# Banded attention: the output mix as three one-pass products of split operands, with the casts on VectorE and GpSimd

## The reference

```python
qkv = (x @ Wqkv.T + bqkv)            # 16 heads of 16; x is layer-normed, 1024 tokens, 256 wide
scores = einsum('bhncd,bhnld->bhncl', qc, kb) / sqrt(d)
attn = softmax(where(band, scores, -inf))
o = einsum('bhncl,bhnld->bhncd', attn, vb)   # weigh the values
return o @ Wout.T + bout             # the output mix; the caller adds x
```

## Time and profile before

| | us |
|---|---|
| runs of the kernel | 3609.21, 3608.74, 3601.73; median 3608.74 |
| the profiled execution | 3606.72 |
| its span in the profile | 3604.9 |
| of it `window_attention` | about 2846 to 3532 |

### The profile page before, as it was taken

One profiled execution on the slowest core, in us unless ns is written; L12 is line 12 of the kernel. 1 busy time (PEld: TensorE's weight loads), 2 busy tenths in 40 slices (PEclk: granted clock), 3 DMA queues, 4 the chain that ended last, 5 costly groups with the idle time before them and its releaser, 6 DMA issues. The chain is left out here.

```text
span 3604.9 us, 123855 instructions
## 1 busy us (share of the span) xinstructions
PE 3338.7 (93%) x48438; PEld 3008.6 (83%) x48438; DVE 2214.2 (61%) x6367; ACT 2105.8 (58%) x6623; POOL 1554.9 (43%) x2318
## 2 busy tenths in 40 slices
PE   8939999789957999899999999999998899999998
PEld 8929999777737999898999899899997677877877
DVE  6675555688775555545544444444444688888887
ACT  5546555455445555444444444444444499999996
POOL 5755565201024665344444444454444533333225
PEclk9969999899978999999999999999999899999999
DMA  4153343511134443500000000000000143333332
GB/s 129 48 169 85 89 97 56 159 48 51 52 136 135 91 95 67 144 3 3 3 3 3 3 3 3 3 3 3 3 3 6 52 129 115 101 105 104 105 96 99
DMA packets 202968, 234.47 MB, mean 65 GB/s; under 512 B 18065, under 2 KB 183073, under 8 KB 202401
## 3 DMA queue, kind: packets, MB, share of 16 engines
q1 hardware_dynamic: 177824, 192.99, 17.1%
q0 software_dynamic: 24576, 33.57, 5.6%
HBM read 147.46 MB, written 79.04 MB: 63 GB/s over the span
## 5 line engine op out<-in xcount | busy, mean ns | idle before, releaser
L2437 ACT ACTIVATE wa_S<-wa_S,wa_top 128x192 f32<-128x192 f32 x1024 | 459.6, 464 | 52.7 <-DVE wa_top L2502 52.6
L1956 DVE TENSOR_TENSOR so_raw<-so_rows,so_masks 128x1024 f32<-128x1024 f32 x256 | 313.5, 1225 | 228.6 <-PE so_rows L1655 219.7
L2035 POOL TENSOR_TENSOR so_more<-so_compact,so_head 128x384 f32<-128x384 f32 x224 | 185.2, 827 | 339.1 <-PE so_bankC L1737 308.4
L2502 DVE CUSTOM_DVE_ANT_0 wa_S<-wa_bank,wa_band 128x192 f32<-128x192 f32 x1024 | 299.5, 349 | 3.9 <-issue 3.9
L1945 DVE SCALAR_TENSOR_TENSOR so_compact<-so_compact,so_bankX 128x96 f32<-128x96 f32 x192 | 48.8, 254 | 355.6 <-PE so_bankX L1773 355.6
L2040 POOL TENSOR_TENSOR so_OT<-so_O,so_OT 128x128 fp32r<-128x128 f32 x256 | 116.9, 456 | 307.9 <-ACT so_OT L1876 307.9
L1870 ACT COPY so_O<-so_bankC 128x128 f32<-128x128 f32 x256 | 68.1, 266 | 308.1 <-PE so_bankC L1737 308.1
L650 POOL DMA_INDIRECT sum_dram<-y,rows x128 | 222.9, 1741 | 29.4 <-issue 27.3
L2348 PE MATMUL wa_bank<-ident,wa_S 128*128 128x128 f32 x1536 | 220.8, 277 | 8.0 <-ACT wa_probT L2444 5.4
L728 ACT ACTIVATE m2e_hT<-m_bank,m2e_bias 128x256 fp32r<-128x256 f32 x256 | 126.8, 495 | 149.7 <-PE m_bank L680 143.2
L728 ACT ACTIVATE m4e_hT<-m_bank,m4e_bias 128x256 fp32r<-128x256 f32 x256 | 126.3, 493 | 150.2 <-PE m_bank L680 145.0
(11 more groups left out here) (449 smaller groups left out, 10030.2 us busy)
## 6 DMA issues: line engine op xcount, KB each, us to landing
m_w_raw<-in_L_ffn_W_dram SPq DMA_DIRECT2D x64, 512.0 KB
wa_V<-wa_V_dram SPq DMA_DIRECT2D x256, 128.0 KB, 2.8
sum_dram<-X SPq DMA_DIRECT2D x16, 1024.0 KB, 4.8
X<-sum_dram SPq DMA_DIRECT2D x16, 1024.0 KB, 8.4
wa_V_dram<-wa_V_new SPq DMA_DIRECT2D x32, 512.0 KB, 4.1
wa_V_rest<-wa_V_dram SPq DMA_DIRECT2D x128, 128.0 KB, 3.0
X<-in_L_attn_a_x_dram SPq DMA_DIRECT2D x8, 1024.0 KB, 11.7
xn_dram<-m2r_xn SPq DMA_DIRECT2D x16, 512.0 KB, 4.5
```

Source lines behind the costliest of these rows:

```text
L1956: nc.vector.tensor_tensor(AB[:, t % 2].rearrange("p h m t -> p h (m t)"), rows4[:, :, 0:2 * P], masks[:].rearrange("p m t -> p (m t)")[:, ...
L2035: nc.gpsimd.tensor_tensor(state[:, t % UT], compact[:, t % UT, :, None, :].broadcast_to([P, 3, HG, DK]), head[:, None, :, None].broadcast_ ...
L2437: nc.scalar.activation(S[:, n % 2, z], S[:, n % 2, z], ACT.Exp, bias=top[:, n % 2, z:z + 1], scale=-1.0, accum_out=sums[:, i % 2, SET * c ...
L2502: nc.vector.tensor_tensor_reduce(out=S[:, n % 2, z], in0=bS[g][:, eo * SPAN:(eo + 1) * SPAN], in1=band[:], scale=-(D ** -0.5), scalar=3e38 ...
```

## The change

`woT` becomes a pair of `float32r` tiles, a high and a low part; the weights are loaded into a piece of `S` that isn't in use yet, ACT casts the high part after its items of the first batch and DVE subtracts for the low part after its own. PE waits for that (`w_ready` 3) before its first `scores`. `OT` becomes such a pair too. In `weighed` the product is written over `RT`; a third DVE instruction casts it to the high part, and a new instruction on POOL, `low_O`, subtracts for the low part; that one now gives `O_ready`. `weigh` waits for the new `O_read`. The mix is six `float32r` products (three pairs of parts, two chunks) in place of two float32 ones.

```diff
-        woT = sb("woT", [P, HC, HID])
+        woT = sb("woT", [P, 2, HC, HID], F32R)
...
-        wT_raw = S[:].rearrange("p a z k -> p (a z k)")[:, 0:HC * 3 * HID].rearrange("p (c r) -> p c r", c=HC)
+        raw_weights = S[:].rearrange("p a z k -> p (a z k)")
+        wT_raw = raw_weights[:, 0:HC * 3 * HID].rearrange("p (c r) -> p c r", c=HC)
+        woT_raw = raw_weights[:, HC * 3 * HID:HC * 4 * HID].rearrange("p (c r) -> p c r", c=HC)
...
-        OT = sb("OT", [P, 2, HC, P])
+        OT = sb("OT", [P, 2, 2, HC, P], F32R)
...
-                sp.dma_start(woT[:], R.outT_dram).then_inc(s_["out_loaded"], 16)
+                sp.dma_start(woT_raw, R.outT_dram).then_inc(s_["out_loaded"], 16)
...
+                def low_O(i):
+                    pool.wait_ge(s_["O_high"], i + 1)
+                    nc.gpsimd.tensor_tensor(OT[:, i % 2, 1].rearrange("p c t -> p (c t)"), RT,
+                                            OT[:, i % 2, 0].rearrange("p c t -> p (c t)").bitcast(F32), ALU.subtract).then_inc(s_["O_ready"], 1)
...
                         low_xT(position(b + 1, 2 * j))
+                    if 1 <= i <= NT:
+                        low_O(i - 1)
...
                     if c == 0 and i >= 1:
-                        pe.wait_ge(s_["O_ready"], i)
+                        pe.wait_ge(s_["O_read"], i)
...
                 def mix(i):
                     pe.wait_ge(s_["O_ready"], i + 1)
-                    for c in range(HC):
-                        last = nc.tensor.matmul(bO[:, HID:2 * HID], OT[:, i % 2, c], woT[:, c, :], start=(c == 0), stop=(c == HC - 1))
+                    steps = [(u, v, c) for u, v in PARTS for c in range(HC)]
+                    for n, (u, v, c) in enumerate(steps):
+                        last = nc.tensor.matmul(bO[:, HID:2 * HID], OT[:, i % 2, u, c], woT[:, v, c, :], start=(n == 0), stop=(n == len(steps) - 1))
...
-                pe.wait_ge(s_["out_loaded"], 16)
+                pe.wait_ge(s_["w_ready"], 3)
...
+                act.wait_ge(s_["out_loaded"], 16)
+                nc.scalar.copy(woT[:, 0], woT_raw).then_inc(s_["w_high"], 1)
...
                 def weighed(i):
                     dve.wait_ge(s_["RT_done"], i + 1)
+                    if i >= 1:
+                        dve.wait_ge(s_["O_ready"], i)
                     nc.vector.tensor_copy(RT, bO[:, HID:2 * HID]).then_inc(s_["RT_ready"], 1)
                     dve.wait_ge(s_["RT_ready"], i + 1)
-                    nc.vector.tensor_tensor(OT[:, i % 2].rearrange("p c t -> p (c t)"), bO[:, 0:HID], RT, ALU.mult
-                                            ).then_inc(s_["O_ready"], 1)
+                    nc.vector.tensor_tensor(RT, bO[:, 0:HID], RT, ALU.mult).then_inc(s_["O_read"], 1)
+                    dve.wait_ge(s_["O_read"], i + 1)
+                    if i >= 2:
+                        dve.wait_ge(s_["out_done"], i - 1)
+                    nc.vector.tensor_copy(OT[:, i % 2, 0].rearrange("p c t -> p (c t)"), RT).then_inc(s_["O_high"], 1)
...
+                dve.wait_ge(s_["w_high"], 3)
+                nc.vector.tensor_tensor(woT[:, 1], woT_raw, woT[:, 0].bitcast(F32), ALU.subtract).then_inc(s_["w_ready"], 1)
                 for n in range(SETS + 6):
```

More of the change, by code:

```diff
@@ L2138, in window_attention @@
         top, sums, share = sb("top", [P, 2, SET]), sb("sums", [P, 2, H]), sb("share", [P, 2, H])
-        OT = sb("OT", [P, 2, HC, P])
+        OT = sb("OT", [P, 2, 2, HC, P], F32R)
         names = """loaded qkv_loaded out_loaded zeroed V_zeroed V_edges step var_ready std_ready scaled xn_ready item_done act_item dve_item qm_ready S_done masked
-                   prob_ready T_done T_act T_dve PV_done share_ready share_spread RT_done RT_ready O_ready out_done y_ready
+                   prob_ready T_done T_act T_dve PV_done share_ready share_spread RT_done RT_ready O_read O_high O_ready out_done y_ready
                    x_ready w_high w_ready xT_low""".split()
```

## The result

| | us |
|---|---|
| before, median of 9 runs | 3606.35 (3601.73 to 3609.21) |
| changed, median of 9 runs | 3615.14 (3608.62 to 3616.61) |
| ratio, changed to before | 1.0024, 95% interval 1.0013 to 1.0034 |
| profiled executions | 3606.72 and 3615.26, spans 3604.9 and 3613.4 |

The change makes the kernel slower by 8.8 us, 0.24%, as forecast (3616; by the sum +9.3 us).

What follows compares the result with a forecast made beforehand. ACT was taken as the bound except in n = 8 to 15 of seven batches, bound by a closed DVE-PE loop. Loop 4.2, held cast 2.3, start 1.9 and end 0.93 gave +9.3 us, 3616 us; range 3604 to 3625.

Steps and rivals of the forecast that it cites:

- What bounds the stage: In n = 8 to 15 of seven batches, a closed loop of mix, DVE with `weighed`, `scores`, PE; elsewhere ACT.
- Rivals 3: DVE isn't the loop's tighter side: casts are free, the mix's gain stays; -1.9 us, 3604.8 us; chance 0.15.
- 4 (PE bounds everywhere): PE is the bound in every n and each of 64 mixes gains: -8 us, 3598.7 us; chance 0.05.
- The cast, +0.33 us: In `weighed`, a DVE cast of 0.29 us puts 0.33 us more on DVE ahead of the next mask.
- Rival 5: The cast runs at the one-to-one rate, 0.42 us; the mix gains only 0.11: +15 us, 3621.7 us; chance 0.15.
- The mix, -0.17 us: On PE, six `float32r` products take 0.85 us where the float32 mix took 1.02, a gain of 0.17 us.
- The loop, +4.2 us: In n = 8 to 15 of seven batches, each of 28 pairs of n grows by 0.15 us: +4.2 us.
- the held cast, +2.3 us: At n = 7, `low_xT` on POOL holds DVE's cast; 0.33 us reaches the mix of n = 8, seven times: +2.3 us.
- Rival 2: The cast isn't held by POOL: +7.0 us, 3613.7 us; chance 0.15.
- `low_O` on POOL, nothing: 64 subtractions of 0.73 us on POOL cost nothing, except at the very end.
- The start, +1.9 us: Before the first `scores`, the subtraction for the weights' low part delays the first mask; ACT bounds from there: +1.9 us.
- The end, +0.93 us: Cast and `low_O` make the last mix 1.10 us later, less 0.17 for the faster mix: +0.93 us.

Runs made afterwards that it cites:

- the cast alone: Kernel before plus one DVE cast of 128x256 behind the product of `weighed`, into a tile nobody reads; 3617.18 us beside 3606.28, ratio 1.0031.
- the mix alone: Changed kernel without cast and `low_O`, the product written straight to the high part, which all six products read; 3604.26 us beside 3606.28, ratio 0.9995.
- two products: Changed kernel with a second DVE product from PSUM writing the high part in place of the cast; 3611.97 us beside 3606.28, ratio 1.0015.
- the cast behind the masks: Changed kernel with the cast moved behind the eighth mask of the same n; 3605.27 us beside 3606.28, ratio 0.9997.
- the late subtraction at the start: Changed kernel with the weights' low-part subtraction behind the masks of n = 0, PE's wait at the first mix; 3612.56 us beside 3605.31, ratio 1.0015.

## Why the prediction was right, point by point

**What bounds the stage.** Right, and it is shown, not only argued: a cast added alone lengthens the pair by its 0.33 us, a second one by 0.16 of its 0.18, and the same cast behind the last mask by nothing. Rivals 3 (DVE has slack) and 4 (PE bounds everywhere) are refuted by the cast alone and the mix alone.

**The cast, +0.33 us.** Right to the hundredth: cast 0.294 us in n = 9 to 15. Rival 5 with its 0.42 us is refuted.

**The mix, -0.17 us.** It was -0.15: from the first start to the bias addition 0.91 us against 1.06. The products start 0.112 to 0.124 us apart in n = 8 to 14, 0.119 on average, where I took 0.113. A pair in the loop so costs 0.18 and not 0.15.

**The loop, +4.2 us, and the held cast, +2.3 us.** Together 6.5 were forecast. In the trace n = 8 to 15 of seven batches take 5.6 us more and the other n, the first apart, 0.7. How they divide is read from bias addition to bias addition. With two products, where nothing is held, the four steps of two n from n = 8 to 16 take 4.8 us more over seven batches than in the kernel before, but the step behind them (n = 16 to 18) takes 1.0 less, so that 3.9 us are left of the loop's term and not 28 x 0.18 = 5.0; that this lies so near 4.2 is partly luck, since the pair was sized too low and what comes back behind the loop was allowed for by rounding down only. In the changed kernel all these steps take 6.2 us more; the 2.3 between the two is the held cast. The held casts took 1.11 to 1.39 us, most of them less than the 1.3 to 1.5 that I had named; at n = 7 I had 1.45 for the mask's delay, and the row shows (3249.44 - 3247.94) - 0.35 = 1.15, since `low_xT` had started 0.3 us before the product's end. Even so the mix of n = 8 came 0.29 to 0.33 us later in six of the seven batches, counted from the first exponent of n = 7, and 0.59 in the first (0.33 forecast), and taking the holding away gave 2.5 us there. That the cast is held at all was an assumption there, from an instruction with two SBUF inputs; the two kinds of cast, 0.29 us alone and 1.11 or more beside `low_xT`, and the two products that nothing holds now show it. The Trainium skill, page "SBUF — State Buffer", section "SBUF: two separate sides", has this as an exclusive lock that a float32 copy between SBUF tensors takes too: the trace agrees, for a cast to `float32r` as well, and the one that waits ends some 0.15 us after the one that it waited for. Rival 2 is refuted.

**`low_O` on POOL, nothing.** Right: the kernel with the cast behind the masks has the same `low_O`, and its pair is as short as that of the mix alone. It counts at the end only, as forecast: PE waits for it once, 2.1 us, at the last tile.

**The start, +1.9 us.** The term that I mis-sized. The wait itself was +1.75, but 0.83 came back. Timelines of the changed kernel:

```profile
2879.91 0.68 DVE L2560 TENSOR_TENSOR wa_woT<-wa_S,wa_woT 128x512 fp32r<-128x512 f32 x1
...
2880.65 0.93 PE L2334 MATMUL wa_bank<-wa_KT,wa_QM 32*64 32x192 f32 x32 [2.42 <-DVE wa_woT L2560]
...
2881.67 0.35 DVE L2514 CUSTOM_DVE_ANT_0 wa_S<-wa_bank,wa_band 128x192 f32<-128x192 f32 x1 [1.08 <-issue]
```

The half-clock stretch in which the loop over n starts is 6.8 us long and began 2.2 to 2.3 us behind the start of the last value items in both kernels; work that is shifted to later by 1.75 us does less of itself in it. I had named this as the unknown of the term, with 1.5 us either way, and should have read from the item of n = 1 at half clock which way it would go. Net +0.9.

**The end, +0.93 us.** It was +1.5, and 0.7 of that is the clock. The changed kernel:

```profile
3535.65 0.29 DVE L2541 CAST wa_OT<-L 128x256 fp32r<-128x256 f32 x1
...
3536.03 0.72 POOL L2247 TENSOR_TENSOR wa_OT<-L,wa_OT 128x256 fp32r<-128x256 f32 x1 [2.62 <-DVE wa_OT L2541]
...
3536.80 1.65 PE L2395 MATMUL wa_bank<-wa_woT,wa_OT 128*128 128x256 f32 x6 [2.11 <-POOL wa_OT L2247]
```

The mix starts 1.61 us after its product, against 0.48 before: +1.13, as worked out (1.10). But it then takes 1.65 us where the one before took 1.13: PE had been idle 2.11 us, and the granted clock of 3536.8 to 3538.5 is 0.50, the level of 1.2 GHz, where the last mix of the kernel before still had 1.00. I had subtracted 0.17 for a faster mix. But the idle time doesn't settle it. With the late subtraction at the start PE had been idle as long, and the granted clock was 1.00:

```profile
3544.37 0.97 PE L2395 MATMUL wa_bank<-wa_woT,wa_OT 128*128 128x256 f32 x6 [2.11 <-POOL wa_OT L2247]
```

In the mix alone PE had been idle only 0.98 us, and the last mix met 0.50. So the 0.7 us between the two clocks can't be put down to the change; at full clock, as in the kernel with the late subtraction, the end is +0.8.

**The sum.** The stage: +0.9 at the start, +6.3 in between, +1.5 at the end, 8.7 us; forecast 1.9 + 6.5 + 0.93. The start came out 1.0 us lower than forecast and the end 0.6 higher, the latter by the clock that the last mix happened to meet. So that the sum is better than its terms is in part luck; the main term, the loop with the held cast, was right by its mechanism.

## What to carry to other kernels

Before a faster product is bought with work on another engine, find the closed loop of waits and see on which side of its hand-over the new work stands: here 0.29 us of DVE cost 0.33 us a turn ahead of the mask that `scores` wait for, and nothing behind it. An SBUF-to-SBUF cast on DVE that takes 0.29 us alone took up to 1.39 beside a GpSimd instruction of 1.3; a product that reads PSUM, slower alone, was the better one. And measure such a change by a length inside the stage: the kernel's total scatters by as much as the effect.

## What the runs showed of the hardware that I had not expected

A group of `float32r` products begins slower behind float32 transposes: in the mixes there the first two starts are 0.20 us apart and the others 0.112 to 0.124, while behind a `float32r` item all five steps are of the latter size. So a mix behind a transpose item takes 0.99 us to the bias addition and one behind a product item 0.91. What slows the first step isn't shown; behind an idle PE, at full clock, it is 0.22.

The clock at the stage's start is worth as much as some edits. In the executions of the mix alone and of the two products a second stretch of 3.4 us at half clock came some 18 us after the start of the loop (windows of the two products: us, busy of PE, PEld, DVE, ACT, POOL; clock 1.00, then 0.50):

```profile
2900.50:2903.90 3.40, 1.66 (x22) 1.31 (x12) 2.81 (x15) 3.40 (x14) 1.64 (x2) 1.00 0.92 318
2903.90:2907.30 3.40, 3.40 (x18) 2.39 (x25) 0.04 (x1) 2.76 (x12) 1.32 (x2) 0.50 0.65 182
```

PE was busy through it, but just before it had been idle 1.74 us, waiting for `low_xT`. That can't be all: the changed kernel and the kernel before have the same idle time of 1.74 us at that place, and their clock stays at 1.00. The stretch made one step between exponents 6.9 us long where the other batches have 5.4. Whether the edits make such a stretch more likely can't be said from one profile of each; that is left open.
